# Row transfers and the eviction split in the first attention of a two-layer kernel

## The reference, cut to what matters

```
x: (1, 2048, 128), H = 16 heads of HD = 8
q, k, v = split((x @ w_qkv).reshape(1, 2048, 16, 24), 3)
scores  = einsum('bhqd,bhkd->bhqk', q, k) / sqrt(8)
w       = relu(scores)
attn    = w / (sum(w, over k) + 1e-6)
out     = attn @ v, all heads side by side, @ w_out + b_out, then a residual and a layer norm
```

## Time and profile before

| | us |
|---|---|
| median of three timed runs | 1501.8 |
| profiled execution, its own time | 1497.75 |
| its span, first to last instruction | 1495.9 |
| TensorE busy | 1338.2 (89%) |
| VectorE busy | 1026.3 (69%) |
| ScalarE busy | 730.9 (49%) |
| GpSimd busy | 705.5 (47%) |
| mean granted TensorE clock, share of full | 0.957 |

### The profile page before, as it was taken

The page is one execution under the profiler, slowest core; times in us unless marked ns, Lnnn a source line. Parts: engine busy times, 40 slices in busy tenths (PEclk is TensorE's granted clock), DMA queues, the critical chain, the costliest instruction groups (busy, mean ns, idle before and its releaser), DMA issues.

```text
span 1495.9 us, 25720 instructions
## 1 busy us (share of the span) xinstructions
PE 1338.2 (89%) x9954; PEld 701.7 (47%) x9954; DVE 1026.3 (69%) x1612; ACT 730.9 (49%) x1167; POOL 705.5 (47%) x521
## 2 busy tenths in 40 slices
PE   5398279999999999798999999999999999999895
PEld 3377212222222223655555555555656555555552
DVE  6875158888888887577676676676676666766762
ACT  2043057787777777443444444444434344444331
POOL 1100104201010010155878877867777678778686
PEclk9598679999999999999999999999999999999997
DMA  4210013000000000000000000000000000000000
GB/s 172 76 54 13 35 65 96 2 1 2 2 2 1 2 1 2 1 1 1 1 2 1 1 1 1 1 1 1 1 1 1 1 1 1 1 1 1 8 8 14
DMA packets 18182, 21.57 MB, mean 14 GB/s; under 512 B 7672, under 2 KB 15888, under 8 KB 16528
## 3 DMA queue, kind: packets, MB, share of 16 engines
q1 hardware_dynamic: 17776, 17.84, 3.5%
q10 hardware_dynamic: 288, 2.10, 0.3%
HBM read 14.70 MB, written 5.24 MB: 13 GB/s over the span
## 4 chain that ended last, share of the span: by engine, by line
PE 40%; DVE 10%; ACT 3%; POOL 2%; issue 1%; POOLq 0%; ACTq 0%
PE psum L1690 12%; PE psum L1668 11%; DVE part_max L1829 4%; PE psum L1620 4%; DVE inv L1850 4%; PE psum L1671 3%; ACT prob L1772 2%; PE psum L1652 2%; PE psum L1607 2%; POOL acc L1587 2%; PE psum L1643 2%; PE psum L1598 1%; DVE z L1853 1%; PE psum L1600 1%; PE psum L1599 1%; PE psum L1625 1%
## 5 line engine op out<-in xcount | busy, mean ns | idle before, releaser
L1587 POOL TENSOR_TENSOR acc<-acc,prob 128x1024 f32<-128x1024 f32 (+3 forms) x264 | 523.8, 1984 | 89.0 <-ACT prob L1772 57.4
L1772 ACT ACTIVATE prob<-psum 128x1024 f32<-128x1024 f32 (+1 forms) x320 | 283.6, 898 | 353.6 <-PE psum L1671 346.8
L1829 DVE TENSOR_REDUCE part_max<-psum 128x2 f32<-128x1024 f32 (+2 forms) x320 | 336.8, 1064 | 169.8 <-PE psum L1620 85.4
L578 DVE TENSOR_SCALAR w<-psum 128x512 f32<-128x512 f32 x472 | 304.9, 686 | 94.1 <-PE psum L433 79.7
L529 ACT ACTIVATE w<-psum 128x512 f32<-128x512 f32 x552 | 293.6, 600 | 121.3 <-PE psum L433 84.3
L453 PE MATMUL psum<-w,v_cols 128*32 128x512 f32 x2048 | 274.1, 608 | 0.0
L1690 PE MATMUL psum<-prob,v_pair 128*64 128x512 f32 (+3 forms) x1280 | 251.9, 536 | 5.7 <-POOL prob L1557 5.7
L1668 PE MATMUL psum<-q_hi,k_hi 64*128 64x512 f32 (+3 forms) x640 | 139.0, 430 | 30.7 <-DVE part_max L1829 21.2
L1690 PEld LDWEIGHTS psum<-prob,v_pair 128*64 128x64 f32 x1280 | 88.2, 138 | 151.0 <-issue 135.8
L1620 PE MATMUL psum<-k_hi,q_hi 64*128 64x512 f32 (+3 forms) x640 | 132.4, 410 | 5.8 <-DVE part_max L1829 4.3
L1850 DVE RECIPROCAL inv<-psum 128x512 f32<-128x512 f32 x32 | 107.3, 3353 | 41.4 <-PE psum L1643 41.4
(11 more groups left out here) (278 smaller groups left out, 1437.6 us busy)
## 6 DMA issues: line engine op xcount, KB each, us to landing
parts_dram<-parts SPq DMA_DIRECT2D x4, 1024.0 KB, 4.7
q_rows<-parts_dram SPq DMA_DIRECT2D x16, 128.0 KB
k_rows<-parts_dram SPq DMA_DIRECT2D x16, 128.0 KB
x<-in_L_attn_x SPq DMA_DIRECT2D x4, 256.0 KB, 4.0
mask<-in_L_ffn_attention_mask SPq DMA_DIRECT2D x1, 1024.0 KB, 5.4
x_high<-parts_dram SPq DMA_DIRECT2D x8, 128.0 KB
x_low<-parts_dram SPq DMA_DIRECT2D x8, 128.0 KB
q_rows<-parts_dram ACTq DMA_DIRECT2D x8, 128.0 KB
```

The lines of the kernel that those rows point to most:

```text
L578: nc.vector.tensor_scalar(w[:, s % WR, 2 * m + 1, :], pair_bank[n % RING][1], 0.0, None, ALU.max)\
L1587: nc.gpsimd.tensor_tensor(sums, sums, prob[:, s % PR, :, q0:C], ALU.add).then_inc(summed, 1)
L1772: nc.scalar.activation(prob[:, s % PR, :, q0:C], unit_both[n % RING][:, :, q0:C], ACT.Exp, scale=SCALE)\
L1829: nc.vector.tensor_reduce(part_max[:, :, i, c], unit_both[n % RING][:, :, 0:cols], AX_X, ALU.max)\
```

## The change

It does three things. First, `prepare` writes the parts to two DRAM tensors of another order: `q_dram` (dimension, part, position) and `k_dram` (head, part, dimension, position). With it a group of four heads is loaded with one transfer of 1024 KB for k and four of 256 KB for q, 5 transfers and not 16; the rows of a head lie in another order, the same for q and k. Second, all groups are issued by SyncE: in `attention0` group 2, then group 3; ScalarE issues none. Third, `SPARE`, `ON_ACT` and the counts made from them are gone: in each of the 512 pairs ScalarE evicts one tile and VectorE one.

```diff
-LOADS = 2 * PARTS * GH
+LOADS = GH + 1
...
-                    sp.dma_start(sh.parts_dram[m, n], parts[:, m, n, :].bitcast(F32)).then_inc(parts_stored, 16)
+                    to = sh.q_dram[:, n, :] if m == 0 else sh.k_dram[:, n, :, :]
+                    sp.dma_start(to, parts[:, m, n, :].bitcast(F32)).then_inc(parts_stored, 16)
...
-        for n in range(PARTS):
-            rows = slice(h * ROWS0 + n * PARTS * HD0, h * ROWS0 + (n + 1) * PARTS * HD0)
-            queue.dma_start(q_rows[rows, :].bitcast(F32),
-                         sh.parts_dram[0, n, head, :].unsqueeze(0).to_broadcast([PARTS, HD0, S]))\
-                .then_inc(loaded, 16)
-            queue.dma_start(k_rows[rows, :].bitcast(F32), sh.parts_dram[1, :, head, :]).then_inc(loaded, 16)
+        q_parts = sh.q_dram[head].rearrange("j n s -> (j n) s")
+        queue.dma_start(q_rows[h * ROWS0:(h + 1) * ROWS0, :].bitcast(F32),
+                        q_parts.unsqueeze(0).to_broadcast([PARTS, PARTS * HD0, S])).then_inc(loaded, 16)
+    k_parts = sh.k_dram[group * GH:(group + 1) * GH].rearrange("h n j s -> (h n j) s")
+    queue.dma_start(k_rows[:, :].bitcast(F32),
+                    k_parts.unsqueeze(1).to_broadcast([GH * PARTS * HD0, PARTS, S])).then_inc(loaded, 16)
...
-        SPARE = [s for s in range(STEPS)
-                 if s % T == DIVIDE and s >= T or s in AFTER and AFTER[s][1] in DVE_FULL or s < G * T and s % T == 12]
-        ON_ACT = [2 * s + 1 for s in SPARE]
...
+            load_rows(sp, sh, 2, q_rows[2], k_rows[2], rows_loaded[2])
             load_rows(sp, sh, 3, q_rows[3], k_rows[3], rows_loaded[3])
...
-                    pe.wait_ge(act_relu, ACTS[n - RING])
-                    pe.wait_ge(dve_relu, DVES[n - RING])
+                    pe.wait_ge(act_relu, n - RING + 1)
+                    pe.wait_ge(dve_relu, n - RING + 1)
...
         @block.scalar
         def _(act):
-            load_rows(act, sh, 2, q_rows[2], k_rows[2], rows_loaded[2])
...
-                    for i in range(2 if n in ON_ACT else 1):
-                        nc.scalar.activation(w[:, s % WR, 2 * m + i, :], pair_bank[n % RING][i], ACT.Relu)\
-                            .then_inc(act_relu, 1)
+                    nc.scalar.activation(w[:, s % WR, 2 * m, :], pair_bank[n % RING][0], ACT.Relu)\
+                        .then_inc(act_relu, 1)
...
-                    if n not in ON_ACT:
-                        dve.wait_ge(scored, n + 1)
-                        nc.vector.tensor_scalar(w[:, s % WR, 2 * m + 1, :], pair_bank[n % RING][1], 0.0, None, ALU.max)\
-                            .then_inc(dve_relu, 1)
+                    dve.wait_ge(scored, n + 1)
+                    nc.vector.tensor_scalar(w[:, s % WR, 2 * m + 1, :], pair_bank[n % RING][1], 0.0, None, ALU.max)\
+                        .then_inc(dve_relu, 1)
```

More of the change, by code:

```diff
@@ L367, in attention0 @@
         AFTER = {s: (c, s - first) for first, c in JOIN.items() for s in range(first, first + G * T)}
-        DVE_FULL = (SUM,) + STATS + (REFINE,) + STATS_X + (REFINE_X,)
-        SPARE = [s for s in range(STEPS)
-                 if s % T == DIVIDE and s >= T or s in AFTER and AFTER[s][1] in DVE_FULL or s < G * T and s % T == 12]
-        ON_ACT = [2 * s + 1 for s in SPARE]
[L372 to L375, removed]
         block = ctx.enter_context(nc.Block())
@@ L439, in weigh @@
                 qc, group = divmod(turn, G)
-                pe.wait_ge(act_relu, ACTS[2 * s + 1])
-                pe.wait_ge(dve_relu, DVES[2 * s + 1])
+                pe.wait_ge(act_relu, 2 * s + 2)
+                pe.wait_ge(dve_relu, 2 * s + 2)
                 if kt == 0:
@@ L1935, in build @@
         sh.bank = [sh.psum[:, b, :] for b in range(8)]
-        sh.parts_dram = nc.dram_tensor("parts_dram", [2, PARTS, D, S], F32, kind="Internal").ap()
+        sh.q_dram = nc.dram_tensor("q_dram", [D, PARTS, S], F32, kind="Internal").ap()
+        sh.k_dram = nc.dram_tensor("k_dram", [H, PARTS, HD0, S], F32, kind="Internal").ap()
         with ExitStack() as layer0:
```

## The result

The changed kernel takes 1477.62 us (median of 4 runs, 1472.34 to 1483.17) against 1501.43 us (4 runs, 1497.62 to 1502.35): a ratio of 0.9847, 95% interval [0.9804, 0.9889]. It is faster by 24 us or 1.5%. 1474 us was forecast, 1463 to 1485 as the range.

A forecast was written before the change was run, and what follows sets the result against it. ScalarE's issuing pause came first, then TensorE bounds the loop, with VectorE nearly as hard. 1497.75 - 38.1 (start) + 12.2 (tiles) = 1471.9 us; 1474 was taken as the middle of two run levels, range 1463 to 1485.

The forecast's parts named there:

- The pause: Start of `attention0`: ScalarE's first eviction waits behind its issuing of group 2; with no issues there, 36.1 us are gained.
- The clock at the start: First steps of `attention0`: they need not run at 1.2 GHz, 2.0 us more gained, 38.1 us in all.
- The transfers: Loads for `attention0`: a group takes 22 to 34 us, no wait at step 32 or 48, cost 0.
- The stores in `prepare`: Stores at another pitch: taken as 0, between -4.7 and +4.7 us, as packets and bytes are the same.
- The 40 tiles: `attention0` loop: VectorE's late first tiles delay TensorE, costing 12.2 us, with bounds 0 and 24 us.
- division (most turns): Loop: division takes VectorE 0.83 us, of which 0.60 stalls TensorE, 15 times, 9.0 us.
- variance at 22, step before it had stalled: Loop, two steps behind a division: TensorE is already late, so the variance's 0.26 us goes, -0.8 us in all.
- refined root at 50, transposes behind: Loop, step 50: transposes (0.58 us) leave 0.27 of the root's stall, the division behind takes most back; 0.1 us in all.
- The tiles cost nothing: Rival, `attention0` loop: throughput alone counts, VectorE has 0.23 us a step free; 1459.7 us, chance 0.09.
- every tile in full: Rival, `attention0`: each of 40 tiles costs 0.60 us, 24 us, and the clock falls at the start; 1485.7 us, chance 0.09.
- One DMA engine: Rival, `attention0` loads: k transfer on one engine, TensorE waits 32 us at steps 32 and 48; 1504 us, chance 0.03.
- ScalarE not freed: Rival, start of `attention0`: the pause is something else, for example its code, and stays; 1510 us, chance 0.02.

The follow-up runs named there:

- move only: Kernel before, its 16 transfers a group and layout kept, with group 2 issued by SyncE instead of ScalarE: 1474.71 us against 1499.27, ratio 0.9837.
- fewer on ScalarE: Changed kernel with the 40 tiles back on ScalarE and group 2 issued by ScalarE in 5 transfers: 1466.53 us against 1499.27, ratio 0.9788.
- k stored as before: Changed kernel, but k in the old DRAM order and read back in 8 transfers a group: 1470.51 us against 1497.18, ratio 0.9819.
- both directions of the swap: Kernel before with the 40 tiles given back to VectorE, 1508.16 us; changed kernel with them back on ScalarE, 1463.48 us; each against 1499.27.
- tiles only: Kernel before with the 40 tiles given back to VectorE and nothing else: 1508.16 us against 1499.27, ratio 1.0058.
- k stored like q: Changed kernel with k stored in the order dimension, part, position and read back in 8 transfers a group: 1470.94 us in one run.

## Why the prediction was right, by its steps

**The pause.** Right in kind and in size: the 36.1 us of issuing are gone. That ScalarE's issue time was the cause is shown by two experiments from two sides (move only, fewer on ScalarE).

**The clock at the start.** Wrong by 2 us. I kept the full 38.1 us because "TensorE now pauses under 1 us at a time", and expected a clock of 1.00 throughout. The start took 8.94 us and not 6.87, 36.0 gained and not 38.1. The clock fell to 1.2 GHz for over 6 us, with TensorE busy for 0.93 of the 2 us of the window in which it fell. The pause that I left out is that between the blocks: TensorE stood idle for 2.12 us ahead of its first scores, as the bracket of its first row shows. In all six other kernels in which ScalarE's evictions start at once the start takes 8.4 to 9.1 us, with the clock at 1.2 GHz for 3.4 to 6.8 us in it, so it is no accident of one run. That the low clock makes up the whole 2 us is argued: no run has a start at full clock. Not tried: filling the pause between the blocks with other matmuls.

**The transfers.** No wait in the changed kernel, as forecast. The bound was too kind, though: from 2.11 us an issue I made 61 GB/s, but the queue doesn't keep that pace (in "move only" issues of 5.66 and 6.73 us stand between those of 2.11), and the mean over two groups was 51 GB/s. With k transfers at the old rate a group would have been late for step 48, as "move only" shows; my "34 us a group" should have been 41. What saves the changed kernel is that the k transfer runs on many engines (a DMA share of 0.94); "k stored as before", with a share of 0.47, shows that fewer would have done.

The Trainium skill's rule on the number of engines ("DMA: Bandwidth & Descriptors", section "Why a DMA increments its semaphore by 16 and not by 1") agrees with this trace on both sides: 0.94 for the k transfer, 0.12, which is two of sixteen, for q alone.

**The stores in `prepare`.** Wrong, by 3.6 us. I took 0 between -4.7 and +4.7 "as packets and bytes are the same". They are, and the k stores still took 7.8 us and not 4.7. The range held it, the value didn't.

**The 40 tiles.** 12.2 us were forecast, 10.1 measured, in both directions of the swap. The rule was right place by place (excess of the step over 1.44 us, forecast and measured in the changed kernel):

| extra work | forecast | measured |
|---|---|---|
| division (most turns) | 0.60 | 0.45 |
| sum | 0.38 | 0.36 |
| statistics, steps 15 and 42 | 0.17 | 0.13, 0.14 |
| statistics, steps 19 and 38 | 0 | 0 |
| variance at 22, step before it had stalled | 0 | 0.02 |
| refined root at 26 | 0.85 | 0.85 |
| refined root at 50, transposes behind | 0.27 | 0.25 |
| four tiles at kt = 12 | 0 | 0 |

Only the division was mis-sized by more than 0.05 us: 15 x 0.15 = 2.2 us, about the whole difference of 2.1. I had read its length from 276.06 to 276.89, but in that kernel the next eviction could not start earlier. Its scores started at 276.27, and the first eviction of a step starts 0.61 us behind the start of its scores (206.96 and 207.57 in the earlier trace rows): 276.88. The distance held 0.14 us of waiting that the view does not mark as idle. In the changed kernel, where the next tile is ready, it is 248.69 - 248.00 = 0.69, and 0.69 - 0.23 = 0.46 is the stall.

**`routed0`** took 2.5 us more in the changed kernel's profile, for which I had no term. It is not a fixed cost of the change: the three other kernels with the same 6.1 us gap have a `routed0` of 125.7, 126.0 and 126.2 us. What it goes with in all ten profiles is the last stretch of `routed0` in which TensorE's clock stands at 1.2 GHz, which begins at 133 to 139 us of the span:

| last low stretch, us | kernels | `routed0`, us |
|---|---|---|
| 10.2 | six | 125.5 to 126.3 |
| 13.7 | before, tiles only, k stored like q | 127.1 to 127.5 |
| 20.5 | changed | 129.6 |

What sets its length I did not isolate. The four runs of the changed kernel go in order with the clock too: mean clocks of 0.970, 0.969, 0.965 and 0.961 and times of 1472.34, 1475.49, 1479.74 and 1483.17 us. So the clock probably makes the wide spread of its times, but only one of the four was profiled.

The sum over the steps in us, measured less forecast: start +2.1, stores +3.6, tiles -2.1, `routed0` +2.5, rest and what lies between the blocks and around the span +1.8; 7.8 in all, which is 1479.74 - 1471.9. The medians lie nearer, 1477.62 against 1474, and in part by luck: the excess that I took for the divisions cancels what I left out at the start, and the profiled run of the changed kernel lies 2.1 us above its median, while that of the kernel before lies 3.7 below.

**The rivals.** "The tiles cost nothing" is refuted by the tiles alone; "every tile in full" as well (10.1, not 24). "One DMA engine" did not occur, but its consequence, a group late for step 48, did in "move only", at 10.6 us of waiting. "ScalarE not freed" is refuted by its timeline.

## What to carry to other kernels

An engine that computes should not issue a row of transfers ahead of its work: here each issue was cheap for the first nine, and then the engine paid, as I read it, the drain of the queue. Count the issues against what is in flight, and check which engines a transfer is spread over before moving it, since a late arrival takes the gain back.

Free time on an evicting engine is worth nothing if its release is only just in time: look at the distance from the start of an eviction to the start of the matmul that needs the bank. The 40 tiles handed to the idle engine bought 10 us in the loop here, and no other stage shows a cost. And the length of a piece of work is read where something waits behind it; elsewhere the distance to the next start hides idle time.

## What the runs showed of the hardware that I had not expected

- The first issues in a row took 0.6 us each of the issuing engine, later ones 2.11 us with one queue at work and 4.3 us with two, which is 61 GB/s in all either way: the engine seems to be held until the queue has drained one transfer.
- Storing the same 128 rows of 8 KB landed in 4.7 us in two orders of the DRAM tensor (part, dimension and dimension, part) and in 7.8 us (median of the two k stores) in the order head, part, dimension.
- From the start of a 128x512 eviction by VectorE to the start of the matmul that waited for it are 0.84 us, though the eviction itself lasts 0.69 and the next one starts after 0.60.
- TensorE's clock can fall to 1.2 GHz just after TensorE has started to work, behind a pause of 2.12 us, and stay there while it works: 0.50 in windows with 1.70, 2.00 and 2.00 of 2.00 us busy.
